# A language-model layer with local and full attention and a mixture of experts, on one core: masks merged, one turn per shift, expert biases in bf16, and the first scores ahead of batch 1's projections

## The chip, the cores and the metric

The kernel runs on one core of a Trainium2 chip. The metric is the device time of one execution in microseconds. Times of before are the median of three runs and one further, profiled execution.

## What is computed

Four sequences of 512 tokens, 256 columns. The embedding rows are gathered; then local attention (16 heads of 16 columns, windows of 128 tokens, each query window sees its own window causally and the one before) on the normalised rows; then, again on normalised rows, full attention with 16 heads plus a mixture of 8 experts of which each token uses 2.

```python
h = W_tok[x]                                      # (4, 512, 256)
h = h + local_attention(layernorm(h)) @ Wo + bo   # window 128, one back, causal
xn = layernorm(h)
q, k, v = split(xn @ W_qkv + b_qkv)
attn = softmax(q @ k.T / sqrt(16)) @ v            # full, 16 heads
gate = softmax(xn @ W_gate + b_gate)
top_g, top_i = top_k(gate, 2)
combine = sum(one_hot(top_i, 8) * top_g[..., None], axis=2)
expert_out = einsum('bsd,edf->bsef', xn, W_experts) + b_experts
h = h + attn + einsum('bsef,bse->bsf', expert_out, combine)
```

## The kernel before

Everything is written by hand in five instruction streams, one per engine, which wait for one another on semaphores. There are eight stages, `STAGES`: local attention of batches 0, 1, 2, full of 0, local of 3, full of 1, 2, 3. Ahead of them stands an opening (`START`) of `START_SLOTS` half slots. A stage has 16 slots (units), 4 groups of 4 heads with 4 key tiles each, and a slot two half slots.

Softmax needs each row's maximum first. So for every head TensorE (PE) computes row scores (`row_scores`, tile SC, two banks) from stacked bf16 parts of q and k: each fp32 value is split in three bf16 parts, and `PRODUCTS` says which parts meet in the 96 rows of QS and KS. In a local stage a bank holds two windows; each window is one matmul (L1487) and one more (L1490) that adds a causal mask by the identity. VectorE (DVE) takes the negated maxima of a bank (`maxima`, L989, L994, L997). When a group of four heads has its maxima, DVE splits them into two bf16 parts (`shift`, L1006, L1008), PE turns them (`turn_shift`, L1419, four transposes, one per row tile, into 8 rows of 512), ScalarE (ACT) copies the bank to shiftT (`copy_shift`, L831), and two DMAs bring shiftT into rows 96 and 97 of QS (`shift_rows`, L515 on SP; for the first group L898 on ACT's queue). Only then can PE compute the transposed scores of that group (`scores`, tile ST, L1504 full, L1510 local), ScalarE takes exponentials (prob, L851, L854), GpSimd masks the local ones (L722), and PE multiplies by V (`times_v`, tile OB, L1531). Row scores run ahead of the transposed ones by `LEAD` heads, 7 or 6. Their place in a slot is given by quarters.

All else is a job: `prep_jobs` says at which step of a batch's preparation (`PREPS` gives the half slot of step 0) PE turns x (`turn_x`, L1296), projects q and k (`project_qk`, L1309, four jobs of two fp32 matmuls of 512 columns) and v (`project_v`, L1324), turns comb, the tokens' weights of the experts (`turn_comb`, L1332), multiplies it by the experts' biases (`expert_bias`, L1339, jobs "eb"), and so on. Jobs use the banks R0 and R1 in turn, and `claim` waits until the reader of the job two before has finished. q and k parts go to memory (`write_parts`, L508) and come back stacked (`stack`, L478). comb is ready at L1073 on DVE, three steps before its turn; `add_biases` (L1128) adds the eb banks to h.

In the opening `START_HEADS` puts row scores of batch 0's first seven heads between the projections of batch 1: heads 0 and 1 in half slot 21, 2 and 3 in 22, then one each. PE runs 8 warming matmuls on the way (`keep_warm`, L1290, fp32, 256 columns), two of them right before stage 0. Group 0's shift is turned in half slot 23.

## Time and profile before

| | us |
|---|---|
| median of 3 runs | 618.83 (614.81 to 619.05) |
| profiled execution | 616.8 |
| its span (first to last instruction) | 615.1 |
| PE busy | 557.4 (91%), granted clock 0.972 |
| DVE busy | 423.3 (69%) |
| ACT busy | 296.1 (48%) |
| GpSimd (POOL) busy | 182.1 (30%) |
| stage 0 begins | 51.4 |
| stages 1 to 7 begin | 103.7, 155.2, 211.6, 281.8, 350.3, 447.3, 534.9 |

A stage begins where the timeline shows its first transposed score. Busy time is the time in which an engine had an instruction under way; PE's matmuls overlap, and an fp32 matmul shows as two. In the timeline and the chain "x4" is a run of four such records. A granted clock of 1 is 2.4 GHz, of 0.5 it is 1.2 GHz.

### The profile page before, as it was taken

To read this page: it belongs to the slowest core of one execution; us is meant where nothing else is said; L and a number is where in the kernel's file an instruction comes from. 1 tells how busy PE (TensorE), PEld (TensorE's weight loads), DVE (VectorE), ACT (ScalarE), POOL (GpSimd) and SP (SyncE) were. 2 spreads that over 40 slices of the span, in tenths; PEclk is the share of its full clock that TensorE was granted. 3 is DMA by queue.
4 is the path that set the end of the run, shared out by engine and by line. 5 is a ranking of instruction groups with operands and counts; after the bars stand their busy time and mean duration, and the time that the engine had idled before them with its cause. 6 is when DMAs were issued, how large, how long until landed. Compare 5 with 4: busy or idle time off the path is not lost.

```text
span 615.1 us, 9977 instructions
## 1 busy us (share of the span) xinstructions
PE 557.4 (91%) x3453; PEld 300.0 (49%) x3453; DVE 423.3 (69%) x941; ACT 296.1 (48%) x558; POOL 182.1 (30%) x237
## 2 busy tenths in 40 slices
PE   3978899989999898898988899989999899999996
PEld 2445555655655343444543455544535555544452
DVE  6867566758687879576577777756876665677842
ACT  0324455546444665475363354524655455444444
POOL 6436544315222501022132133301133341043201
PEclk9998899999899999999896799999999999999999
DMA  6365334224221443351224123403258578223311
GB/s 186 107 197 173 103 117 126 78 63 121 87 87 53 132 125 101 92 152 55 69 85 141 58 68 125 129 19 97 62 167 240 164 235 254 70 60 104 112 52 36
DMA packets 43521, 69.24 MB, mean 113 GB/s; under 512 B 7368, under 2 KB 36688, under 8 KB 40784
## 3 DMA queue, kind: packets, MB, share of 16 engines
q1 hardware_dynamic: 39088, 55.62, 30.2%
q0 software_dynamic: 4224, 12.59, 6.5%
q8 instruction: 28, 0.46, 0.3%
q10 hardware_dynamic: 160, 0.40, 0.2%
q14 instruction: 21, 0.17, 0.1%
HBM read 45.25 MB, written 23.07 MB: 111 GB/s over the span
## 4 chain that ended last, share of the span: by engine, by line
PE 72%; DVE 17%; issue 4%; DMA 2%; ACT 2%; SPq 1%; POOL 1%; DVEq 0%; ACTq 0%
PE OB L1531 13%; PE R L1411 9%; PE R L1309 9%; PE SC L1482 8%; PE ST L1504 6%; PE R L1324 5%; DVE neg_max L989 4%; PE SC L1487 4%; PE R L1397 3%; PE ST L1510 3%; PE R L1426 2%; PE R L1357 2%; PE SC L1490 2%; DVE neg_max L997 2%; PE R L1296 1%
## 5 line engine op out<-in xcount | busy, mean ns | idle before, releaser
L989 DVE TENSOR_REDUCE neg_max<-SC 128x1 f32<-128x512 f32 x256 | 170.9, 686 | 84.8 <-PE SC L1482 84.0
L851 ACT ACTIVATE prob<-ST 128x512 f32<-128x512 f32 x256 | 136.8, 598 | 123.5 <-PE ST L1504 122.9
L1531 PE MATMUL OB<-prob,VS 128*32 128x512 f32 (+2 forms) x1024 | 109.7, 502 | 0.1
L1482 PE MATMUL SC<-KS,QS 96*128 96x512 bf16 x256 | 98.7, 394 | 8.2 <-DVE neg_max L989 6.1
L854 ACT ACTIVATE prob<-ST 128x512 f32<-128x512 f32 (+1 forms) x128 | 68.4, 543 | 73.2 <-PE ST L1510 72.7
L722 POOL TENSOR_SCALAR_AFFINE_SELECT prob<-prob 128x512 f32<-128x512 f32 x64 | 41.0, 642 | 146.1 <-ACT prob L854 145.9
L1504 PE MATMUL ST<-QS,KS 98*128 98x512 bf16 x256 | 78.1, 382 | 2.0 <-ACT prob L851 1.9
L997 DVE TENSOR_REDUCE neg_max<-SC 128x2 f32<-128x512 f32 x64 | 44.0, 688 | 26.1 <-PE SC L1490 26.0
L1487 PE MATMUL SC<-KS,QS 96*128 96x256 bf16 (+1 forms) x256 | 55.3, 270 | 3.7 <-DVE neg_max L994 2.7
L994 DVE TENSOR_REDUCE neg_max<-SC 128x1 f32<-128x128 f32 (+1 forms) x128 | 39.5, 350 | 23.4 <-PE SC L1490 23.2
L1490 PE MATMUL SC<-mask_q,ident_bf 128*128 128x128 bf16 x256 | 51.7, 226 | 0.0
L1482 PEld LDWEIGHTS SC<-KS,QS 96*128 96x128 bf16 x256 | 25.1, 98 | 50.8 <-DVE neg_max L989 33.6
L1510 PE MATMUL ST<-QS,KS 98*128 98x256 bf16 (+1 forms) x256 | 48.5, 273 | 1.2 <-DMA QS<-shiftT 1.2
L708 POOL TENSOR_TENSOR parts<-rest,parts 128x512 bf16<-128x512 f32 x32 | 37.4, 1169 | 40.9 <-ACT parts L797 24.3
L792 ACT ACTIVATE parts<-R,qk_bias 128x512 bf16<-128x512 f32 x32 | 22.0, 687 | 54.9 <-PE R L1309 54.9
L1504 PEld LDWEIGHTS ST<-QS,KS 98*128 98x128 bf16 x256 | 24.6, 98 | 31.9 <-ACT prob L851 11.6
L732 POOL TENSOR_TENSOR h<-h,AO 128x256 f32<-128x256 f32 x15 | 10.9, 727 | 97.9 <-DVE AO L1031 70.3
L1487 PEld LDWEIGHTS SC<-KS,QS 96*128 96x128 bf16 x256 | 25.3, 101 | 28.0 <-DVE neg_max L994 10.9
L1531 PEld LDWEIGHTS OB<-prob,VS 128*32 128x32 f32 x1024 | 20.5, 110 | 37.0 <-issue 34.0
L962 DVE SCALAR_TENSOR_TENSOR rest<-R,qk_bias,parts 128x512 f32<-128x512 f32 x32 | 23.9, 747 | 18.1 <-ACT parts L792 16.4
L1309 PE MATMUL R<-xT_full,w_qkv 128*128 128x512 f32 x64 | 33.0, 608 | 3.0 <-DVE VS L974 3.0
L1151 DVE SCALAR_TENSOR_TENSOR h<-R,comb,h 128x256 f32<-128x256 f32 x64 | 27.8, 475 | 8.8 <-PE R L1411 8.8
(148 smaller groups left out, 800.5 us busy)
## 6 DMA issues: line engine op xcount, KB each, us to landing
scratch<-parts SPq DMA_DIRECT2D x96, 128.0 KB
QS<-scratch SPq DMA_DIRECT2D x42, 256.0 KB, 3.3
KS<-scratch SPq DMA_DIRECT2D x42, 256.0 KB, 3.6
...
```

The source lines that it names most:

```text
L851: act.activation(prob[:, u % 2, e, :], src[:, :], ACT.Exp, scale=SCALE).then_inc(s_prob, 1)
L854: act.activation(prob_local[:, u % 2, u // 2 % 2, 2 * e:2 * e + 2, 0:w], src[:, :].rearrange("p (i w) -> p i w", i=2)[:, :, 0:w], ACT.Exp, ...
L989: dve.tensor_reduce(own_max[:, i, head:head + 1], bank[:, :], AX.X, ALU.max, negate=True).then_inc(s_max, 1)
L997: dve.tensor_reduce(own_max[:, 2:4, head], bank[:, :].rearrange("p (w k) -> p w k", w=2), AX.X, ALU.max, negate=True).then_inc(s_max, 1)
L1309: mm = pe.matmul(bank[:, :], w, xT_of(p)[:, c, :], start=(c == 0), stop=(c == NC - 1))
L1411: mm = pe.matmul(bank[:, t % 2 * D:(t % 2 + 1) * D], xT_full[b % 2][:, c, t * P:(t + 1) * P], w_exp[n % W_RING][:, c, :], start=(c == 0), ...
L1482: pe.matmul(bank[:, :], Q[0:SHIFT_ROW, head, i * P:(i + 1) * P], K[0:SHIFT_ROW, head, :], start=True, stop=True).then_inc(s_sc_ps, 1)
L1487: pe.matmul(bank[:, first:last], Q[0:SHIFT_ROW, head, w * P:(w + 1) * P], K[0:SHIFT_ROW, head, max(w - 1, 0) * P:(w + 1) * P], start=(w % ...
L1490: mm = pe.matmul(bank[:, last - P:last], ident_bf[:, :], mask_q[:, :], start=False, stop=(w % 2 == 1), skip_group_check=True)
L1504: mm = pe.matmul(bank[:, :], K[0:KROWS, g * GH + e, keys], Q[0:KROWS, g * GH + e, :], start=True, stop=True)
L1510: mm = pe.matmul(bank[:, i * 2 * P:i * 2 * P + w], K[0:KROWS, head, keys], Q[0:KROWS, head, kt * P:kt * P + w], start=(i == 0), stop=(i == 1),
L1531: mm = pe.matmul(OB[VW * i:VW * (i + 1), columns], VS[s % 3][:, kt, v:v + VW], p_of, start=(kt == 0), stop=(kt == NT - 1), skip_group_chec ...
```

## The change

Four things at once.

1. *Masks.* The two mask matmuls of a bank become one of 256 columns (two blocks of 128 with the mask read twice by a stride of 0), after both score matmuls.
2. *Shift.* The two parts are stored as part, head, tile, so that one transpose of 32 columns makes 32 rows of 128; ScalarE copies 32x128; each DMA brings 16 rows of 128 into one row of QS.
3. *Expert biases.* comb and the biases are each split in three bf16 parts; six products of parts are stacked in a contraction of 48 rows, so that turn and product are bf16. comb is split by four GpSimd operations after L1073 (`split_comb`), the biases by four more in stage 0 (`split_biases`), and six DMAs stack them at the start of stage 1. exp_bias now lies in the xs buffers, which are free then.
4. *Opening.* Heads 0 to 3 get half slots 20 to 23, one each, 4 in 24, and 5 and 6 in 25; the shift is turned in 24. Batch 1's projections of q and k are at steps 10, 11, 14, 16 instead of 9, 11, 13, 15, and V at 19 and 21 instead of 14 and 16, the opening is one half slot shorter, and the two warming matmuls before stage 0 go.

```diff
-START_STACK, START_SHIFT = 15, 23
-START_HEADS = {21: (0, 1), 22: (2, 3), 23: (4,), 24: (5,), 25: (6,)}
+START_STACK, START_SHIFT = 15, 24
+START_HEADS = {20: (0,), 21: (1,), 22: (2,), 23: (3,), 24: (4,), 25: (5, 6)}
...
-START_SLOTS, VS_ONES = 27, 5
+START_SLOTS, VS_ONES = 26, 5
...
-Q_STEPS = {"first": (9, 10, 11, 12), "later": (9, 11, 13, 15)}
-V_STEPS = {"first": (13, 14), "second": (14, 16), LOCAL: (10, 12), FULL: (8, 8, 9, 10)}
+Q_STEPS = {"first": (9, 10, 11, 12), "second": (10, 11, 14, 16), "later": (9, 11, 13, 15)}
+V_STEPS = {"first": (13, 14), "second": (19, 21), LOCAL: (10, 12), FULL: (8, 8, 9, 10)}
...
+SPLIT_STEP = 20
+
+BIAS_PRODUCTS = ((0, 0), (0, 1), (0, 2), (1, 0), (1, 1), (2, 0))
...
-        shift = sb("shift", [P, NT, 2 * GH], BF16)
-        shiftT = sb("shiftT", [2 * GH, T], BF16)
+        shift = sb("shift", [P, 2, GH, NT], BF16)
+        shiftT = sb("shiftT", [2 * GH * NT, P], BF16)
...
-                    sp.dma_start(QS[s % 2][SHIFT_ROW + j:SHIFT_ROW + j + 1, g * GH:(g + 1) * GH, :],
-                                 shiftT[j * GH:(j + 1) * GH, :]).then_inc(s_shrow, 16)
+                    sp.dma_start(shift_row(s, g, j), shiftT[j * GH * NT:(j + 1) * GH * NT, :]).then_inc(s_shrow, 16)
...
+            def stack_biases():
+                sp.wait_ge(s_bias_parts, 4)
+                for n, (_, a) in enumerate(BIAS_PRODUCTS):
+                    sp.dma_start(bias_stack[n * E:(n + 1) * E, :], bias_parts[:, a, :]).then_inc(s_bias_stack, 16)
...
+            def split_comb(b):
+
+                n = at(b, 4, 0)
+                pool.wait_ge(s_comb, b + 1)
+                if b > 0:
+                    pool.wait_ge(s_comb_ps, b)
+                rows = comb[b % 2][:, :, :]
+                pool.tensor_copy(comb_parts[:, :, 0:3, :], rows.unsqueeze(2).to_broadcast([P, NT, 3, E]))\
+                    .then_inc(s_comb_parts, 1)
+                pool.wait_ge(s_comb_parts, n + 1)
+                pool.tensor_tensor(comb_rest[:, :, :], rows, comb_parts[:, :, 0, :], ALU.subtract)\
+                    .then_inc(s_comb_parts, 1)
...
             def turn_comb(b):
-                bank = claim(("comb", b, 0))
-                pe.wait_ge(s_comb, b + 1)
+                turned = claim(("comb", b, 0))[:, :].bitcast(BF16)
+                pe.wait_ge(s_comb_parts, at(b, 4, 4))
                 for t in range(NT):
-                    mm = pe.transpose(bank[0:E, t * P:(t + 1) * P], comb[b % 2][:, t, :], ident[:, :])
+                    mm = pe.transpose(turned[0:len(BIAS_PRODUCTS) * E, t * P:(t + 1) * P],
+                                      comb_parts[:, t, :, :].rearrange("p n e -> p (n e)"), ident_bf[:, :])
                 mm.then_inc(s_comb_ps, 1)
...
-                    mm = pe.matmul(bank[:, (t % 2) * D:(t % 2 + 1) * D], combT[:, t * P:(t + 1) * P], exp_bias[:, :],
+                    mm = pe.matmul(bank[:, (t % 2) * D:(t % 2 + 1) * D], combT[:, t * P:(t + 1) * P], bias_stack[:, :],
...
-                for t in range(NT):
-                    mm = pe.transpose(turned[0:2 * GH, t * P:(t + 1) * P], shift[:, t, :], ident_bf[:, :])
-                mm.then_inc(s_shT_ps, 1)
+                pe.transpose(turned[0:2 * GH * NT, 0:P], shift[:, :, :, :].rearrange("p j i t -> p (j i t)"),
+                             ident_bf[:, :]).then_inc(s_shT_ps, 1)
...
-                    mm = pe.matmul(bank[:, last - P:last], ident_bf[:, :], mask_q[:, :], start=False,
-                                   stop=(w % 2 == 1), skip_group_check=True)
-                mm.then_inc(s_sc_ps, 1)
+
+                own = bank[:, :].rearrange("p (w k) -> p w k", w=2)[:, :, (i > 0) * P:((i > 0) + 1) * P]
+                pe.matmul(own, ident_bf[:, :], mask_q[:, :].unsqueeze(1).to_broadcast([P, 2, P]), start=False,
+                          stop=True, skip_group_check=True).then_inc(s_sc_ps, 1)
...
-            keep_warm(2)
             pe.wait_ge(s_ones, 5)
```

PE's stream where the first row scores stand, in the opening, before (R<-ident,xn_local is batch 1's turned x, R<-xT_local,w_q its first q projection, SC<-KS,QS the scores of a window, SC<-mask_q,ident_bf its mask):

```order
L1296 MATMUL R<-ident,xn_local 128x128 x8
L1309 MATMUL R<-xT_local,w_q 128x512 x2
L1487 MATMUL SC<-KS,QS 128x128
L1490 MATMUL SC<-mask_q,ident_bf 128x128
L1487 MATMUL SC<-KS,QS 128x256
L1490 MATMUL SC<-mask_q,ident_bf 128x128
```

The same place in the changed kernel, PE's stream from batch 1's turned x on:

```order
L1355 MATMUL R<-ident,xn_local 128x128 x8
L1548 MATMUL SC<-KS,QS 128x128
L1548 MATMUL SC<-KS,QS 128x256
L1553 MATMUL SC<-mask_q,ident_bf 128x2x128
L1548 MATMUL SC<-KS,QS 128x256 x2
L1553 MATMUL SC<-mask_q,ident_bf 128x2x128
L1368 MATMUL R<-xT_local,w_q 128x512
```

Head 0's two banks now stand ahead of the projection, which comes one matmul at a time between the heads, and a bank has three matmuls instead of four.

PE's stream where the opening ends and stage 0 begins (the first ST rows), before:

```order
L1324 MATMUL R<-w_v,xT_local 128x256 x2
L1309 MATMUL R<-xT_local,w_k 128x512 x2
L1290 MATMUL OB<-w_q,ident 128x256 x2
L1510 MATMUL ST<-QS,KS 128x256 x2
L1324 MATMUL R<-w_v,xT_local 128x256 x2
```

The same place in the changed kernel, PE's stream from the opening's last matmul on:

```order
L1368 MATMUL R<-xT_local,w_q 128x512
L1572 MATMUL ST<-QS,KS 128x256 x2
L1548 MATMUL SC<-KS,QS 128x128
L1548 MATMUL SC<-KS,QS 128x256
L1553 MATMUL SC<-mask_q,ident_bf 128x2x128
L1572 MATMUL ST<-QS,KS 128x256 x2
L1368 MATMUL R<-xT_local,w_k 128x512
```

The last k projection and all of V have moved behind the first transposed scores, the warming matmuls are gone.

SP's stream at the same place (scratch<-parts writes parts of q and k, QS<-shiftT is group 1's shift rows, QS<-scratch and KS<-scratch the stack of batch 1), before:

```order
L478 DMA KS<-scratch 32x1x2048 x3
L508 DMA scratch<-parts 8x16x512 x12
L515 DMA QS<-shiftT 1x4x512 x2
L478 DMA QS<-scratch 32x1x4096
L478 DMA KS<-scratch 32x1x4096
```

The same place in the changed kernel, SP's stream:

```order
L495 DMA KS<-scratch 32x1x2048 x3
L525 DMA scratch<-parts 8x16x512 x6
L532 DMA QS<-shiftT 1x16x128 x2
L495 DMA QS<-scratch 32x1x4096
L525 DMA scratch<-parts 8x16x512 x6
```

Group 1's shift rows, and the first piece of batch 1's stack, now go between the two halves of the parts' writes.

## Rows read from the trace of the kernel before

**Rows 1.** Of the page, part 1: busy us (share of the span) xinstructions.
```profile
PE 557.4 (91%) x3453; PEld 300.0 (49%) x3453; DVE 423.3 (69%) x941; ACT 296.1 (48%) x558; POOL 182.1 (30%) x237
```

**Rows 2.** Of the page, part 4: the chain that ended last, share by engine.
```profile
PE 72%; DVE 17%; issue 4%; DMA 2%; ACT 2%; SPq 1%; POOL 1%; DVEq 0%; ACTq 0%
```

**Rows 3.** Windows, stages 4, 5: PE, PEld, DVE, ACT, POOL, clock, DMA, GB/s.
```profile
281.80:350.30 68.50, 59.32 (x391) 29.98 (x389) 47.27 (x117) 28.04 (x53) 16.66 (x23) 0.83 0.29 89
350.30:447.30 97.00, 93.85 (x488) 51.66 (x485) 70.44 (x156) 45.66 (x86) 23.64 (x25) 0.99 0.27 83
```

**Rows 4.** The timeline, PE: start us, us, engine line op out<-in xcount.
```profile
107.51 0.39 PE L1419 MATMUL R<-ident_bf,shift 128*8 128x128 bf16 x4
107.83 0.23 PE L1487 MATMUL SC<-KS,QS 96*128 96x128 bf16 x1
107.90 0.22 PE L1490 MATMUL SC<-mask_q,ident_bf 128*128 128x128 bf16 x1
107.96 0.27 PE L1487 MATMUL SC<-KS,QS 96*128 96x256 bf16 x1
108.07 0.22 PE L1490 MATMUL SC<-mask_q,ident_bf 128*128 128x128 bf16 x1
```

**Rows 5.** The chain: the first and last of 16 shift turns.
```profile
98.01 0.32 PE R L1419 x4
...
588.63 0.20 PE R L1419 x4
```

**Rows 6.** The timeline, ScalarE and its queue (ACTq), the opening.
```profile
27.80 2.20 ACTq L478 DMA_DIRECT2D KS<-scratch  x3
...
43.14 0.57 ACT L831 COPY shiftT<-R 8x512 bf16<-8x512 bf16 x1
43.74 1.82 ACTq L898 DMA_DIRECT2D QS<-shiftT  x2
```

**Rows 7.** The chain, then the timeline of SP and PE: three times shift rows.
```profile
100.20 3.47 DMA QS<-shiftT
...
103.72 0.39 PE L1510 MATMUL ST<-QS,KS 98*128 98x256 bf16 x2 [1.19 <-DMA QS<-shiftT]
...
108.76 1.19 SPq L515 DMA_DIRECT2D QS<-shiftT  x2
...
111.33 0.38 PE L1510 MATMUL ST<-QS,KS 98*128 98x256 bf16 x2
```

**Rows 8.** The chain: eb jobs, the first, and one at half clock.
```profile
157.54 1.05 PE R L1339 x4
...
289.88 1.87 PE R L1339 x4
```

**Rows 9.** The chain: a turn of comb.
```profile
281.10 0.53 PE R L1332 x4
```

**Rows 10.** Groups of instructions, GpSimd, a small operation.
```profile
L660 POOL TENSOR_SCALAR_AFFINE_SELECT tri<-ones_bf 128x128 bf16<-128x128 bf16 x1 | 0.3, 282 | 0.0
```

**Rows 11.** The timeline, DVE and PE, comb of batch 0.
```profile
152.66 0.19 DVE L1073 TENSOR_TENSOR comb<-chosen,grec 128x32 f32<-128x32 f32 x1
...
153.74 0.60 PE L1332 MATMUL R<-ident,comb 128*8 128x128 f32 x4
```

**Rows 12.** The timeline, PE: a moving operand repeated by a stride of 0.
```profile
340.95 0.35 PE L1371 MATMUL R<-sel,ones_bf 128*128 128x64 bf16 x8
```

**Rows 13.** The timeline, DVE, the opening.
```profile
35.95 0.75 DVE L962 SCALAR_TENSOR_TENSOR rest<-R,qk_bias,parts 128x512 f32<-128x512 f32 x1 [4.35 <-ACT parts L792]
36.62 0.61 DVE L994 TENSOR_REDUCE neg_max<-SC 128x1 f32<-128x128 f32 x2
...
37.78 0.62 DVE L994 TENSOR_REDUCE neg_max<-SC 128x1 f32<-128x128 f32 x2
```

**Rows 14.** The chain, the end of the opening.
```profile
48.97 1.72 PE R L1309 x4
50.69 0.86 PE OB L1290 x4
```

More of the change, by code:

```diff
@@ L204, in q_step @@
 def q_step(p):
-    return Q_STEPS["first" if p == 0 else "later"]
+    return Q_STEPS[("first", "second")[p] if p < 2 else "later"]
 def v_step(p):
@@ L741, in prep @@
                             third_part(p, i)
-                    if what == "local" and step == (26 if p == 0 else q_step(p)[3] + 4):
+                    if what == "local" and step == (24 if p == 0 else q_step(p)[3] + 4):
                         add_bo(b)
+                    if what == "full" and step == SPLIT_STEP:
+                        split_comb(b)
                 if what == "route":
@@ L830, in copy_shift @@
                 turned = bank_of(("shift", group, 0))[:, :].bitcast(BF16)
[L831 removed]
+                act.copy(shiftT[:, :], turned[0:2 * GH * NT, 0:P]).then_inc(s_shT, 1)
             def copy_OT(group):
@@ L1005, in maxima @@
                         dve.wait_ge(s_shT_ps, group)
-                    dve.tensor_copy(shift[:, :, 0:GH], own).then_inc(s_sh1, 1)
+                    first, second = (shift[:, j, :, :].rearrange("p i t -> p t i") for j in (0, 1))
+                    dve.tensor_copy(first, own).then_inc(s_sh1, 1)
                     dve.wait_ge(s_sh1, group + 1)
-                    dve.tensor_tensor(shift[:, :, GH:2 * GH], own, shift[:, :, 0:GH], ALU.subtract)\
-                        .then_inc(s_sh, 1)
+                    dve.tensor_tensor(second, own, first, ALU.subtract).then_inc(s_sh, 1)
             def attention_before(s, g):
```

50 lines of the change are left out of this document (42 added, 8 removed).

## The prediction

> **What bounds the kernel now.** I read the busy shares of the page first: TensorE (PE) is busy 91% of the span [rows 1]. That is an average, so next comes the chain that ended last: 72% of it is PE, 17% VectorE (DVE), 4% bare issue, 2% DMA [rows 2]. Work taken off PE is therefore worth something, but not all of it, since now and then DVE's maxima come last. Then the granted clock by stage: 0.99 in stage 5, where PE is busy 97% of the time, and 0.83 in stage 4, where it is busy 87% [rows 3]. A microsecond of PE's stream saved is worth one where the chain holds the instruction, and little elsewhere.
>
> The sum is made against the profiled execution: 616.8 us, of which the span is 615.1. It lies 2 us under the median of the three timed runs (618.83) and between their extremes.
>
> **One turn per shift.** A group's shift was four bf16 transposes of 128 columns with 8 rows out; now it is one with 32 rows out. Beside one another in the timeline, a matmul of 128 bf16 columns begins 0.06 to 0.07 us before its successor (107.83, 107.90, 107.96), one of 256 columns 0.11 us (107.96, 108.07) [rows 4]. The four transposes begin at 107.51 and the next matmul at 107.83. So three go, 3 x 0.056 = 0.17 us, and the switch-over around them, some 0.1 us, stays. There are 32 such turns, but only 16 stand in the chain, the first at 98.01 and the last at 588.63 [rows 5]: 16 x 0.17 = **2.7 us**. At the other 16 something else came last, and I count nothing for them.
> ScalarE's copy of the turned bank goes from 512 elements, 0.57 us [rows 6], to 128. Bounds for it: the 0.57 itself, and a quarter, 0.14. ScalarE is not the bound (2% of the chain), so this counts only through earlier shift rows. DVE's two small operations on the shift now write with a stride; 16 elements cost what starting an operation costs, and I take 0, ends -0.2 and +1 us.
>
> The shift rows leave as 16 pieces of 128 elements (256 bytes) per DMA where there were 4 of 1 KB. The chain names them once as what PE waited for: 3.47 us after the issue, with 1.19 us of waiting before 103.72 [rows 7]. There the shorter turn and copy give back about 0.5 us, and a slower landing could take it away. Value taken: 0, ends -0.5 and +1; the general case is rival 4.
>
> **Expert biases in bf16.** An eb job is two fp32 matmuls of 256 columns, shown as x4 since each passes twice. Seven of the eight stand in the chain: about 1.05 us each at full clock, 1.87 for the one at half clock [rows 8]. As bf16 each matmul takes the 0.11 us of [rows 4], so a job becomes 2 x 0.11 plus 0.08 of switching = 0.3 us: 6 x 0.75 + (1.87 - 0.6) = **5.8 us**. That the contraction goes from 8 rows to 48 changes nothing in the columns streamed; the scores, with 96 rows, take the same 0.11.
>
> The turn of comb was four fp32 transposes, 0.53 us in the chain [rows 9], four times; as bf16 it is 4 x 0.056 plus the switch, 0.32. 4 x 0.21, and a little more for the one at half clock: **1.0 us**.
>
> What is added is on GpSimd: four small operations after comb, each waiting for the one before. The nearest row is an affine select of 128x128, 0.28 us [rows 10]; four of these with short gaps are 1.3 us. For batches 1 to 3 comb is ready 3 us and more before PE turns it, so this is hidden. For batch 0 DVE ends comb at 152.85 and PE turned it at 153.74 [rows 11]; now it can't before 154.2, and PE takes its instructions in order, so row scores, transposed scores and values stand behind it. **-0.5 us**, ends 0 and -1.2 (each operation half as long, or twice). The four operations that split the biases (stage 0, GpSimd) and the six DMA issues that stack them (start of stage 1, SP, 6 x 0.6 = 3.6 us by the two issues of [rows 7] in 1.19) come while GpSimd has nothing due but a mask every slot, and two slots ahead of SP's next shift rows, some 6 us. I count 0; if the SP ones collide, the next group is late once, 1 us.
>
> **Merged masks.** Per bank two mask matmuls of 128 columns become one of 256. The columns are equal and one instruction's own overhead goes: 0.06 + 0.06 becomes 0.11, about 6 ns a bank. 128 banks, of which two thirds are in PE-bound stretches: **0.5 us**. That a moving operand repeated by a stride of 0 runs at full rate is shown by the routing counts, eight such matmuls within 0.35 us [rows 12]. Bounds: 0 and 1.5.
>
> **The opening.** Before, PE projects batch 1's first q, and DVE sits idle 4.35 us until that projection's remainder at 35.95, ahead of its first maximum at 36.62 [rows 13]. Stage 0 begins at 51.4, after a k projection of 1.72 us and the warming matmuls, 0.86 [rows 14]. Now head 0's scores stand ahead of the projection. They can start when batch 1's transposes have ended, shortly before the projection did, and ScalarE's K stack has landed: issued 27.80 to 30.00 [rows 6], its last piece from 29.3 on, and at most 3.5 us from issue to landing as in [rows 7], so 33 or little earlier. A head costs DVE 37.78 - 36.62 = 1.16 us. Four heads and two remainders of 0.75 end at 33.3 + 6.1 = 39.4, shift ready at 39.8 (it was 42.6). Turn and copy to 40.5, ScalarE issues the two rows until 42.3 (1.82 us [rows 6]), and they land at 43.7 to 45.2 (2.0 or 3.5 us after the second issue begins, by the two cases of [rows 7]). DVE's three further heads and one remainder run until 44.0, PE's last scores a head before that. So stage 0 starts at 44.4, 7.0 us earlier. Of this the k projection (1.72) and V's first four fp32 matmuls twice (0.9 each, as long as the four warming ones of the same size) are owed to stage 0; the warming is really gone. 7.0 - 3.5 = **3.5 us**. Bounds: 1 (DVE's idle time merely moves) and 5.
>
> **Sum.** 2.7 + 5.8 + 1.0 - 0.5 + 0.5 + 3.5 = 13.0 us. Outside the opening DVE often follows closely, and where a microsecond of PE goes the next maximum is late instead; by the share of DVE and issue in the chain I take off a fifth of those 9.5 us, 2.0. Forecast 616.8 - 11.0 = 605.8, rounded to **606 us**.
>
> **Rivals.**
> 1. *DVE takes over.* PE gets its two banks for row scores back from DVE's maxima. If half of the chain terms (9.5) turn into that wait and the opening gives only 1 us and the warming matmuls, it is 616.8 - 4.8 - 1.9 = 610. For it: DVE is 17% of the chain [rows 2]. Against it: bias jobs and turns lie among projections, which give DVE time.
> 2. *More than the sum.* In stage 0 PE waits for DVE again and again and its clock is halved twice for 3.4 us; if both go (up to 1.7 us of stream each) and the opening gives 5, it is about 600.
> 3. *The clock, the slower side.* Less PE work leaves PE idle more often. Stage 4 was granted 0.83 at 87% busy, stage 5 0.99 at 97% [rows 3]. If stage 5 alone fell to stage 4's clock, its 93.9 us of PE would take 93.9 x (0.99/0.83 - 1) = 18 us more, and the time be 616.8 - 11 + 18 = 624. It decides from 0.89 on, where it eats the 11 us. Against it: the idle added there is some 2% of the stage.
> The Trainium skill (TensorE: Matmul & The Clock Gate, "The HAM clock gate") puts it generally: the slow clock is the default and activity releases it. The trace agrees in direction; by that rule a kernel that only loses PE work gains less than the columns say.
> 4. *Late shift rows.* SP ends an issue at 109.95 and PE uses the rows at 111.33 without a recorded wait [rows 7]. Through the timeline five or six of the 32 groups are that tight. If 256-byte pieces landed 2.5 us later, each of these would cost 2 us and the next tight ones some: 12 us, nothing gained, 618. Against it: 4 KB is little in any pieces.
> The Trainium skill (DMA: Bandwidth & Descriptors, Specifications) says that pieces under 512 bytes go by read-modify-write and miss the line rate. No run here shows yet what that is worth for 4 KB.
>
> **Numbers.** Forecast 0.62; rival 1 0.17; rival 2 0.11; rival 3 0.06; rival 4 0.04. The range takes in rival 1's 610 with what lies past it, and rival 2's 600: 599 to 613. A measurement of this kernel tells about 1% from no change, that is 612.6 against the median of 618.8: faster 0.80 (the forecast, rival 2 and half of rival 1), same 0.15, slower 0.05.
>
> **What would show it.** The first score of stage 0 near 44.4; DVE's 4.35 us idle before its first maximum down to about 1.5; an eb job 0.3 us and a turned shift 0.15 in the chain; less than 1 us of waiting at batch 0's turn of comb; at most one wait for shift rows over 1 us; stages 1 to 7 shorter by 0.5 to 2 us each. Wrong if PE's waits for maxima grow by over 5 us, if the granted clock after 350 us falls below 0.97, or if stage 0 starts before 46 and its end still comes less than 2 us earlier.

## The result, and the profile after

The changed kernel takes 602.85 us (median of 4 runs, 601.53 to 603.44) against 618.11 for the kernel before: a ratio of 0.975, 95% interval 0.970 to 0.979. In experiment e5 the same kernel took 603.71 against 618.66, ratio 0.976 (0.971 to 0.981). Over its ten runs the median is 603.1. The forecast was 606, within 599 to 613. Two runs, one of e11 with 658.2 us (granted clock 0.835) and one of the kernel before with 1338.5 us beside e5 to e8, lie far above all others and are left out of the medians below.

The profiled execution is 602.96 us with a span of 601.2. First the page of the changed kernel, busy times and then the chain by engine, for [rows 1, 2]:

```profile
PE 538.9 (90%) x3209; PEld 282.9 (47%) x3209; DVE 424.4 (71%) x941; ACT 285.4 (47%) x558; POOL 188.2 (31%) x257
...
PE 67%; DVE 20%; issue 5%; DMA 4%; ACT 2%; SPq 1%; POOL 1%; ACTq 0%; DVEq 0%
```

PE lost 244 instructions and 18.5 us of busy time, more than the span lost (13.9), and DVE's share of the chain went from 17 to 20%.

Then the windows by stage, from one first ST matmul to the next (start:end, length, PE, PEld, DVE, ACT, POOL busy, granted clock, DMA share, GB/s). The kernel before, the opening, stage 0 and stage 2; its stages 4 and 5 are [rows 3]:

```profile
0.00:51.39 51.39, 35.85 (x152) 20.98 (x153) 34.95 (x66) 13.71 (x22) 27.38 (x48) 1.00 0.57 168
51.39:103.72 52.33, 46.99 (x390) 27.76 (x388) 35.30 (x84) 25.96 (x51) 27.65 (x36) 0.93 0.43 132
155.18:211.62 56.44, 52.42 (x397) 29.90 (x393) 41.49 (x94) 27.22 (x52) 18.61 (x26) 0.97 0.27 83
```

The changed kernel, the same three and stages 4 and 5:

```profile
0.00:50.78 50.78, 33.74 (x120) 18.60 (x121) 34.63 (x64) 11.31 (x19) 27.38 (x48) 0.93 0.58 167
50.78:101.08 50.30, 46.33 (x358) 26.85 (x356) 36.62 (x87) 26.31 (x53) 29.65 (x40) 1.00 0.46 140
152.45:205.55 53.10, 48.58 (x363) 26.87 (x359) 41.36 (x92) 25.92 (x52) 18.59 (x26) 1.00 0.29 86
275.00:338.19 63.19, 51.82 (x354) 24.94 (x352) 46.98 (x117) 26.54 (x53) 17.62 (x27) 0.89 0.32 97
338.19:435.64 97.45, 94.22 (x477) 51.50 (x473) 70.21 (x156) 44.50 (x86) 24.63 (x29) 0.98 0.27 83
```

The gain sits in a few places: the opening 0.6 us, stage 0 2.0, stage 1 0.1, stage 2 3.3, stage 3 0.7, stage 4 5.3, stage 5 -0.5, stages 6 and 7 2.2 together. The clock column must be read with the length. The kernel before ran at half clock (1.2 instead of 2.4 GHz) for 6.8 us of stage 0, 3.4 of stage 2 and 22.6 of stage 4. The changed one has none in stages 0 and 2 and 13.8 in stage 4, but 6.8 in the opening, where there was none. So a good part of the differences between stages is the clock's. And part of that is not the change's: in the second profile of the changed kernel (e5) stage 4 had 20.6 us at half clock and was 65.6 us long, a gain of 2.9 instead of 5.3, while its opening had none.

The new operations in the chain of the changed kernel (start us, us, what), a turn of the shift, the first turn of comb and two eb jobs, for [rows 5, 8, 9]:

```profile
95.90 0.23 PE R L1480
151.13 0.38 PE R L1391 x4
154.79 0.32 PE R L1401 x2
```

An eb job is 0.32 to 0.39 us where it was 1.05 to 1.87, and a turned shift 0.04 to 0.26, in the chain 15 times.

### The profile page after: what moved, and what is told of

It reads as the page before. It is cut to its first block, busy times and chain, and to the rows that moved or that the text cites. A ratio compares the mean times of both kernels' runs of the same rounds, so it can differ in the third digit from the quotient of the medians.

```text
span 601.2 us, 9518 instructions
## 1 busy us (share of the span) xinstructions
PE 538.9 (90%) x3209; PEld 282.9 (47%) x3209; DVE 424.4 (71%) x941; ACT 285.4 (47%) x558; POOL 188.2 (31%) x257
## 4 chain that ended last, share of the span: by engine, by line
PE 67%; DVE 20%; issue 5%; DMA 4%; ACT 2%; SPq 1%; POOL 1%; ACTq 0%; DVEq 0%
PE OB L1593 12%; PE R L1473 9%; PE R L1368 9%; PE SC L1543 8%; PE ST L1566 6%; DVE neg_max L1048 6%; PE R L1383 4%; PE SC L1548 3%; PE R L1459 3%; PE R L1487 2%; PE R L1419 2%; PE ST L1572 2%; DVE neg_max L1056 2%; PE SC L1553 2%; DVE stats L991 1%
## 5 line engine op out<-in xcount | busy, mean ns | idle before, releaser
L1593 PE MATMUL OB<-prob,VS 128*32 128x512 f32 (+2 forms) x1024 | 107.7, 493 | 0.1
L1548 PE MATMUL SC<-KS,QS 96*128 96x256 bf16 (+1 forms) x256 | 47.4, 268 | 3.9 <-DVE neg_max L1053 1.8
L1543 PEld LDWEIGHTS SC<-KS,QS 96*128 96x128 bf16 x256 | 24.9, 97 | 54.6 <-DVE neg_max L1048 38.1
L1572 PE MATMUL ST<-QS,KS 98*128 98x256 bf16 (+1 forms) x256 | 46.8, 264 | 0.5 <-DMA QS<-shiftT 0.5
L1566 PEld LDWEIGHTS ST<-QS,KS 98*128 98x128 bf16 x256 | 24.8, 98 | 32.2 <-ACT prob L909 11.8
L1548 PEld LDWEIGHTS SC<-KS,QS 96*128 96x128 bf16 x256 | 21.2, 100 | 36.7 <-issue 16.9
L1553 PE MATMUL SC<-mask_q,ident_bf 128*128 128x256 bf16 x128 | 36.0, 281 | 0.0
L1572 PEld LDWEIGHTS ST<-QS,KS 98*128 98x128 bf16 x256 | 25.4, 100 | 18.2 <-issue 11.5
```

Source lines behind the costliest of these rows:

```text
L1543: pe.matmul(bank[:, :], Q[0:SHIFT_ROW, head, i * P:(i + 1) * P], K[0:SHIFT_ROW, head, :], start=True, stop=True).then_inc(s_sc_ps, 1)
L1548: pe.matmul(bank[:, first:last], Q[0:SHIFT_ROW, head, w * P:(w + 1) * P], K[0:SHIFT_ROW, head, max(w - 1, 0) * P:(w + 1) * P], start=(w % ...
L1553: pe.matmul(own, ident_bf[:, :], mask_q[:, :].unsqueeze(1).to_broadcast([P, 2, P]), start=False, stop=True, skip_group_check=True).then_in ...
L1566: mm = pe.matmul(bank[:, :], K[0:KROWS, g * GH + e, keys], Q[0:KROWS, g * GH + e, :], start=True, stop=True)
L1572: mm = pe.matmul(bank[:, i * 2 * P:i * 2 * P + w], K[0:KROWS, head, keys], Q[0:KROWS, head, kt * P:kt * P + w], start=(i == 0), stop=(i == 1),
L1593: mm = pe.matmul(OB[VW * i:VW * (i + 1), columns], VS[s % 3][:, kt, v:v + VW], p_of, start=(kt == 0), stop=(kt == NT - 1), skip_group_chec ...
```

## The experiments

Six runs each, twelve for e12. The kernel before had a median of 618.2 us beside e1 to e4, 618.7 beside e5 to e8, 617.8 beside e9 to e12. The runs of one kernel lie up to 9 us apart, so a difference of two medians is good to about 2 or 3 us; what happened in a stage is read from the traces. The starts of four stages in the profiled executions (first ST matmul of each, us), and where half clock fell (start, length) up to 200 us:

| kernel | median | stage 0 | stage 1 | stage 3 | stage 5 | half clock |
|---|---|---|---|---|---|---|
| before | 618.1 | 51.4 | 103.7 | 211.6 | 350.3 | 58.0 (3.4), 64.8 (3.4), 163.8 (3.4) |
| changed | 602.9 | 50.8 | 101.1 | 205.5 | 338.2 | 34.3 (3.4), 44.5 (3.4) |
| e1 old opening | 604.2 | 50.8 | 101.8 | 206.3 | 338.9 | 59.3 (3.4) |
| e2 four turns | 605.3 | 49.9 | 100.4 | 205.1 | 339.2 | 42.0 (6.8) |
| e3 fp32 biases | 610.2 | 49.6 | 100.2 | 208.8 | 343.0 | 42.0 (6.8), 158.0 (6.8) |
| e4 masks apart | 607.2 | 49.4 | 101.1 | 207.5 | 341.4 | 44.5 (6.8) |
| e5 changed again | 603.7 | 47.2 | 98.2 | 202.9 | 338.2 | none |
| e6 two heads first | 602.1 | 49.0 | 99.5 | 205.4 | 338.8 | 34.9 (3.4), 45.2 (3.4), 198.8 (3.4) |
| e7 warm in waits | 600.3 | 47.5 | 98.8 | 203.2 | 337.7 | none |
| e8 bias of 8 rows | 604.8 | 51.1 | 101.4 | 205.9 | 341.9 | 34.6, 44.9 (3.4 each) |
| e9 stage 4 filled | 605.1 | 47.3 | 98.4 | 202.9 | 341.9 | none |
| e10 two heads and warm | 600.3 | 45.6 | 96.8 | 203.3 | 335.9 | 195.7 (6.8) |
| e11 biases alone | 611.3 | 54.5 | 106.5 | 211.8 | 347.1 | 33.1, 39.9, 67.2 (3.4 each) |
| e12 opening alone | 614.7 | 49.4 | 100.2 | 209.6 | 347.4 | 42.8 (3.4), 158.9 (6.8) |

**e1, the old opening in the changed kernel.**

```diff
-START_STACK, START_SHIFT = 15, 24
-START_HEADS = {20: (0,), 21: (1,), 22: (2,), 23: (3,), 24: (4,), 25: (5, 6)}
+START_STACK, START_SHIFT = 15, 23
+START_HEADS = {21: (0, 1), 22: (2, 3), 23: (4,), 24: (5,), 25: (6,)}
```

with the old START_SLOTS, Q_STEPS and V_STEPS and keep_warm(2) before stage 0.

> The changed kernel with the old opening (heads two at a time from half slot 21, batch 1's V at 14 and 16, two warming matmuls before stage 0). In the profile of the changed kernel stage 0 starts only 0.6 us earlier than before, not 7, and stage 1 2.6 us earlier. Theory A (the new opening is worth what stage 1's start shows): 602.9 + 2.6 minus the masks and turns of stage 0 (0.5) = 605.0, and its own half-clock stretches lie in stage 0 again (58 and 65 us), not in the opening. Theory B (the opening is worth nothing; what stage 1's start shows came by the other three parts and by luck of the clock): 602.9 to 603.5. Theory C (the old opening would now be better, because PE and DVE stand idle together for 3 us in the new one): 601 or less.

Measured: 604.24 (601.24 to 608.74), ratio to before 0.980 (0.976 to 0.983): 1.1 us over the changed kernel's 603.1, less than the runs can settle. In its trace stage 0 starts at the same 50.8, stage 1 0.7 later. What the new opening is worth must come from more traces (below, at the opening).

**e2, four turns per shift.**

```diff
-                pe.transpose(turned[0:2 * GH * NT, 0:P], shift[:, :, :, :].rearrange("p j i t -> p (j i t)"),
-                             ident_bf[:, :]).then_inc(s_shT_ps, 1)
+                for t in range(NT):
+                    mm = pe.transpose(turned[0:2 * GH, t * P:(t + 1) * P], shift[:, t, :], ident_bf[:, :])
+                mm.then_inc(s_shT_ps, 1)
```

> The changed kernel with four transposes per shift, the copy of 8x512 and DMAs of 4 x 1 KB. Chain theory (only the 16 turns that stand in the chain count): +2.7 us, 605.6. Stream theory (all 32 count): +5.4 us, 608.3. Latency theory (the shorter copy and landing matter too, by earlier shift rows where PE waits for them): stage 1's start is 0.5 us later beyond the turns, total +3.5 to +6. If 256-byte pieces land later than 1 KB pieces, the wait before stage 1's first score is shorter here than the one of 3.4 us after the issue ends in the changed kernel.

Measured: 605.31 (603.99 to 606.94), ratio 0.980 (0.977 to 0.983), 2.2 us more. Group by group its trace is 0.11 to 0.25 us longer in eleven of the 32 groups, 1.75 us together, and the same within 0.1 us in the others, except for groups 18 (1.1 more), 22 (1.0), 26 (0.4) and 27 (0.25 less). Group 18 was 1.1 us longer in e5 too, with no edit, so these four say nothing of the turns. So a turn costs what its rows said where PE's stream is the bound, and nothing elsewhere.

**e3, fp32 expert biases.** exp_bias, combT of 8 rows and the fp32 turn of comb again, no split and no stacking:

```diff
-                    mm = pe.matmul(bank[:, (t % 2) * D:(t % 2 + 1) * D], combT[:, t * P:(t + 1) * P], bias_stack[:, :],
+                    mm = pe.matmul(bank[:, (t % 2) * D:(t % 2 + 1) * D], combT[:, t * P:(t + 1) * P], exp_bias[:, :],
```

> The changed kernel with the expert biases and the turn of comb in fp32, without the splitting operations. Theory A (stream): eb jobs and comb turns come back with 5.8 + 1.0 - 0.5 = +6.3 us, 609.2. Rival (half of it turned into waits for DVE): +3, 606. In the profile an eb job is 1.05 us in the chain again, against about 0.3.

Measured: 610.18 (607.59 to 610.75), ratio 0.987 (0.983 to 0.990), 7.1 us more. PE's eb rows of e3, and the window of its group 8:

```profile
153.42 1.13 PE L1349 MATMUL R<-exp_bias,combT 8*128 8x256 f32 x4
157.46 1.55 PE L1349 MATMUL R<-exp_bias,combT 8*128 8x256 f32 x4 [0.99 <-DVE AO L1041]
...
151.15:165.06 13.91, 12.82 (x90) 7.72 (x87) 7.57 (x20) 5.86 (x12) 2.54 (x4) 0.75 0.25 78
```

and the same of the changed kernel:

```profile
154.72 0.39 PE L1401 MATMUL R<-bias_stack,combT 48*128 48x256 bf16 x2
158.03 0.39 PE L1401 MATMUL R<-bias_stack,combT 48*128 48x256 bf16 x2 [0.99 <-DVE AO L1090]
...
152.45:161.81 9.36, 8.34 (x85) 5.35 (x82) 7.33 (x18) 5.77 (x12) 2.16 (x4) 1.00 0.31 89
```

Group 8 is 4.5 us longer. Two jobs of 0.75 us more each explain 1.5; the other 3 fit the 6.8 us at half clock from 158.0 on. The wait of 0.99 us for DVE stands in both. Group 24, which holds two more such jobs, is 3.1 us longer with 3.4 us at half clock from 451.6 on. Half clock stood in group 8 in all three traces with fp32 biases (before, e3, e12) and in none of the eleven others.

**e8, the biases on 8 rows.** Leaves out five of the six products: only the first 8 of the 48 stacked rows are contracted.

```diff
-                    mm = pe.matmul(bank[:, (t % 2) * D:(t % 2 + 1) * D], combT[:, t * P:(t + 1) * P], bias_stack[:, :],
+                    mm = pe.matmul(bank[:, (t % 2) * D:(t % 2 + 1) * D], combT[0:E, t * P:(t + 1) * P], bias_stack[0:E, :],
```

> The changed kernel with the bias product over the first 8 of the 48 stacked rows only; five of the six products of parts are left out. Columns and instruction count are the same. In e3 with fp32 biases of 8 rows the clock was halved for 6.8 us around the eb jobs of stage 2, and here it was not. If that hangs on how few rows of PE the eb matmuls fill, a half-clock stretch comes back in stage 2 and its first group takes 12 us and more; if it hangs on the time that fp32 takes and the waits around it, group 8 takes 9.4 us as now and the time is 602.9.

Measured: 604.82 (601.28 to 608.33). PE's first eb row and the window of group 8:

```profile
155.08 0.39 PE L1401 MATMUL R<-bias_stack,combT 8*128 8x256 bf16 x2
...
152.81:162.18 9.37, 8.36 (x86) 5.35 (x83) 7.33 (x18) 5.77 (x12) 2.17 (x4) 1.00 0.28 85
```

Rows of contraction changed neither the job nor the clock of group 8. What counted there was fp32 against bf16, not 8 rows against 48.

**e4, masks apart.** After each window's scores again a mask matmul of 128 columns of its own:

```diff
-                pe.matmul(own, ident_bf[:, :], mask_q[:, :].unsqueeze(1).to_broadcast([P, 2, P]), start=False,
-                          stop=True, skip_group_check=True).then_inc(s_sc_ps, 1)
+                    mm = pe.matmul(bank[:, last - P:last], ident_bf[:, :], mask_q[:, :], start=False,
+                                   stop=(w % 2 == 1), skip_group_check=True)
+                mm.then_inc(s_sc_ps, 1)
```

> The changed kernel with two mask matmuls per bank. By columns: +0.5 us (6 ns at 128 banks, two thirds of them where PE is the bound), 603.4, not to be told from no change. Rival: each matmul costs more than its columns (its weight load, its instruction): +3 us or more.

Measured: 607.15 (603.49 to 609.23), ratio 0.983 (0.979 to 0.987), 4.1 us more. Its trace is 3.2 us longer than the changed kernel's, with an opening 1.4 us shorter. The longer groups are of three kinds. Thirteen groups are 0.05 to 0.33 longer, 1.6 us together, which I take for the columns' own price. Groups 0 and 16 are 1.0 and 0.7 longer with more half clock (group 16 was 1.25 longer in e5, with no edit). Group 4 is 1.4 longer because group 5's shift rows, issued from 105.8 on, came late. PE's wait in e4:

```profile
109.92 0.39 PE L1571 MATMUL ST<-QS,KS 98*128 98x256 bf16 x2 [1.19 <-DMA QS<-shiftT]
```

That wait is in no other trace of the series (group 4 is 7.4 to 7.6 us long in all of them, 8.8 here). The same rows, issued at the same time, were used 2.1 us after the second issue's begin in the changed kernel and 3.5 us here; one trace doesn't tell whether masks apart bring it. The masks are worth 1.6 us by the groups and perhaps up to 4 by the medians, which is not shown.

**e5, the changed kernel again**, unedited, to see what of its opening repeats.

> The changed kernel itself, on the same chip and in the same hour as the next three. All theories: 602.9, within 601.5 to 604.5, stages as in its first profile except where a half-clock stretch falls otherwise (up to 1.7 us each).

Measured: 603.71 (599.33 to 607.11). PE's wait for the shift and the window up to stage 0, in e5:

```profile
42.65 0.22 PE L1480 MATMUL R<-ident_bf,shift 128*32 128x128 bf16 x1 [3.16 <-DVE shift L1068]
...
28.00:47.20 19.20, 13.41 (x71) 7.34 (x70) 14.34 (x30) 3.83 (x7) 12.14 (x20) 1.00 0.64 190
```

and in the first profile of the same kernel:

```profile
44.67 0.26 PE L1480 MATMUL R<-ident_bf,shift 128*32 128x128 bf16 x1 [3.15 <-DVE shift L1068]
...
28.00:50.78 22.78, 16.52 (x72) 8.63 (x71) 14.46 (x30) 3.83 (x7) 12.03 (x20) 0.85 0.67 192
```

The same work and the same wait of 3.15 us, but the clock 1.00 in the one and 0.85 in the other, and 3.5 us between the starts of stage 0. One execution of the same kernel differs here from another by more than the two openings differ in the mean (2.6 us, below). The lead didn't last: the spans are 601.2 and 601.4 us. e5 gave 0.7 us back in stage 0 and 2.4 in stage 4, where it had the more half clock.

**e6, two heads first.**

```diff
-START_HEADS = {20: (0,), 21: (1,), 22: (2,), 23: (3,), 24: (4,), 25: (5, 6)}
+START_HEADS = {20: (0, 1), 21: (2,), 22: (3,), 23: (4,), 24: (5,), 25: (6,)}
```

> The changed kernel with two heads ahead of the first projection of batch 1 (START_HEADS 20: 0 and 1, 21: 2, 22: 3, 23: 4, 24: 5, 25: 6) and the shift still turned in half slot 24, so that head 4's scores no longer stand behind a turn that waits. Theory A (what holds the new opening back is DVE without row scores: 1.3 us before head 1, 1.1 us before head 4, 1.4 us before head 5, and remainders waited for ahead of maxima): the shift is ready near 40.6 instead of 44.5, stage 0 starts 3 us or more earlier, and the time falls by 2 to 3 us to about 600.5. Theory B (the opening is bound by PE's own stream at the granted clock and by what stage 0 owes anyway): stage 0 may start earlier, but stage 1 starts at 101 as before, 603.

Measured: 602.06 (598.45 to 604.35), ratio 0.971 (0.967 to 0.976). That is 1.0 us under the changed kernel's 603.1, less than the runs can settle. DVE's shift is ready at 42.8 instead of 44.5 and stage 0 starts 1.7 us earlier, with two stretches of half clock as in the changed kernel. DVE's waits between the heads shrank only from 2.95 to 2.4 us (1.27, 1.23 and 0.45 before, rows below, at the opening). Another 0.7 us came because the second remainder now stands behind the shift, and 0.8 because the two operations on the shift themselves ran faster. DVE in e6, then GpSimd (POOL) in e6, then GpSimd in the changed kernel, where the same two operations took 0.52 and 0.65 us from 43.32 on:

```profile
42.34 0.19 DVE L1066 CAST shift<-neg_max 128x16 bf16<-128x16 f32 x1
42.56 0.20 DVE L1068 TENSOR_TENSOR shift<-neg_max,shift 128x16 bf16<-128x16 f32 x1
...
43.31 1.15 POOL L731 TENSOR_TENSOR parts<-rest,parts 128x512 bf16<-128x512 f32 x1 [7.07 <-ACT parts L855]
...
43.07 2.77 POOL L738 TENSOR_TENSOR h<-h,o_bias 128x256 f32<-128x256 f32 x4
```

In e6 GpSimd is idle beside them, in the changed kernel it adds. The new layout of the shift isn't the reason: e12 has the old layout and the new order, and its two operations take 0.51 and 0.65 us.

**e7, warm matmuls in the opening's waits.**

```diff
                 if t == WARM_X:
                     keep_warm(2)
+                if t == 20:
+                    keep_warm(3)
+                if t == 24:
+                    keep_warm(6)
```

> The changed kernel with warming matmuls where PE waits in the opening: three ahead of head 0 (half slot 20), six ahead of the turn of shift 0 (half slot 24). Clock theory (the two half-clock stretches of the opening, at 34 and 44 us, follow PE's waits, and cost it what the new order saves): no half-clock stretch before stage 0, stage 0 starts 1.5 to 3 us earlier, 600.5 to 601.5. Rival (DVE is the bound of the opening, the clock of PE costs nothing there): the stretches go, and the start of stages 0 and 1 moves less than 0.5 us, 603.

Measured: 600.29 (599.35 to 601.39), ratio 0.969 (0.966 to 0.973). The opening has no half clock, stage 0 starts at 47.5, and the median is 2.8 us under the changed kernel's 603.1. All six runs lie within 2.1 us, those of e5 within 7.8; but the first four runs of the changed kernel lay within 1.9 too, so the smaller spread is not shown. PE's wait for the shift went from 3.15 to 0.57 us. Of the seven profiles with the new opening and no remedy, six had half clock in the opening.

**e9, stage 4's waits filled as well.** On top of e7, and likewise 6 matmuls ahead of an eb job and 7 ahead of group 18's turn of O:

```diff
+            def fill(bank, n):
+                for _ in range(n):
+                    pe.matmul(bank[:, 0:P], ident[:, :], ident[:, :], start=True, stop=True)
...
             def turn_shift(group):
-                turned = claim(("shift", group, 0))[:, :].bitcast(BF16)
+                bank = claim(("shift", group, 0))
+                fill(bank, {17: 16, 20: 7}.get(group, 0))
+                turned = bank[:, :].bitcast(BF16)
```

> The kernel of warm matmuls in the opening's waits, and besides: where PE waits for DVE in stage 4 and just before stage 5 it multiplies the identity by itself meanwhile (16 times 128 fp32 columns ahead of group 17's turn of shift, 6 ahead of the second expert bias job of batch 1, 7 ahead of group 18's turn of O, 7 ahead of group 20's turn of shift), in banks that are overwritten next. Nothing of the computation changes. Before it these four waits took 2.27, 0.94, 1.06 and 0.97 us, and stretches at half clock of 6.8 us followed at 279 and at 334. Theory that PE's waits bring the half clock and the half clock costs time there: both stretches go, stage 4 is 60 to 62 us long (65.1 before it), the time 3 to 5 us under the other kernel with warm matmuls (600.3), 596. Rival, DVE is the bound there whatever PE's clock: the stretches may go, but the next maxima come last, stage 4 is 64.5 to 65.5 long, the time within 1 us of 600.3. Second rival: the matmuls outlast the waits and delay the turns; PE's stream grows by 1 us, 601.

Measured: 605.11 (604.06 to 607.97), 4.8 us slower than e7. PE in e9, the fill and its turn, then the window of group 16:

```profile
278.99 3.84 PE L1481 MATMUL R<-ident 128*128 128x128 f32 x32 [2.27 <-DVE h L1187]
282.76 0.23 PE L1488 MATMUL R<-ident_bf,shift 128*32 128x128 bf16 x1
...
272.28:289.33 17.05, 14.17 (x123) 10.02 (x121) 10.62 (x32) 5.50 (x12) 4.51 (x7) 1.00 0.26 76
```

and e7:

```profile
279.36 0.29 PE L1480 MATMUL R<-ident_bf,shift 128*32 128x128 bf16 x1 [2.27 <-DVE h L1187]
...
272.64:286.75 14.11, 10.90 (x80) 5.67 (x77) 10.31 (x32) 5.57 (x12) 4.54 (x7) 0.76 0.29 91
```

The fill stands behind the wait, not in it. The row said so: it names DVE's h (L1187), which reads the bank that the turn claims, and not DVE's shift (L1068). PE waited for a free bank, and so no matmul into that bank can fill the wait. The stretch at half clock after it did go (clock 1.00 instead of 0.76). Since 16 and 6 fp32 matmuls cost 5.4 us there and a wait of 0.94 us behind them went, and the group grew by only 2.9, the half clock had cost some 1.6 us, by this estimate. Group 19, which holds the other two fills, grew by 2.7 us; groups 18 and 20 came out 1.1 shorter each. Whether a fill inside the wait pays wasn't tried: it needs another bank.

**e10, two heads first and three warm matmuls** (the edits of e6, and of e7 at t == 20).

> The changed kernel with two heads' scores (instead of one) ahead of the first half of the second q projection, and three warm matmuls after them; nothing left out. Two heads alone gave 602.1 and warm matmuls alone 600.3, against 603.3 for the changed kernel (mean of its two medians). Theory that the two remedies are of different kinds (DVE's early work, PE's clock) and add up: stage 0 starts at 46.0 to 46.8, no half clock in the opening, time 599 to 599.5. Rival, both remove the same half-clock stretches: stage 0 starts at 47.2 or later, the time is 600 to 601.

Measured: 600.33 (597.76 to 601.96), ratio 0.971 (0.967 to 0.975). Stage 0 starts at 45.6, 1.9 before e7, yet the medians are equal. In the profiled executions the lead is gone where stage 3 begins, and the profile shows where it went. PE in e10:

```profile
193.35 0.39 PE L1543 MATMUL SC<-KS,QS 96*128 96x512 bf16 x1 [0.71 <-DVE neg_max L1048]
195.98 0.61 PE L1543 MATMUL SC<-KS,QS 96*128 96x512 bf16 x1 [0.75 <-DVE neg_max L1048]
...
196.00:200.00 4.00, 4.00 (x20) 1.96 (x21) 1.91 (x3) 0.85 (x2) 2.69 (x5) 0.50 0.09 33
```

and in e7:

```profile
195.32 0.39 PE L1543 MATMUL SC<-KS,QS 96*128 96x512 bf16 x1 [0.71 <-DVE neg_max L1048]
197.96 0.39 PE L1543 MATMUL SC<-KS,QS 96*128 96x512 bf16 x1 [0.75 <-DVE neg_max L1048]
...
198.00:202.00 4.00, 3.66 (x32) 1.66 (x32) 3.27 (x7) 1.51 (x4) 3.12 (x6) 1.00 0.12 38
```

The same two waits at the same place of the program; after them half clock in e10, full in e7, and group 11 is 14.75 us long in the one, 12.73 in the other. Half clock in group 11 stands in both traces with two heads first (e6, 14.15 us, and e10) and in none of the twelve others, so it may belong to this order of the heads; two traces don't settle it. The profiled execution of e10 was 599.98 us long all the same, that of e7 601.39, for e10's stage 4 was 1.9 us shorter, with 13.9 us at half clock against 21.1.

**e11, the biases alone, and e12, the opening alone**, each put into the kernel before, with nothing else changed. e11 makes the edits that e3 undoes:

```diff
-                    mm = pe.matmul(bank[:, (t % 2) * D:(t % 2 + 1) * D], combT[:, t * P:(t + 1) * P], exp_bias[:, :],
+                    mm = pe.matmul(bank[:, (t % 2) * D:(t % 2 + 1) * D], combT[:, t * P:(t + 1) * P], bias_stack[:, :],
```

> The kernel before with the bf16 expert biases alone (split, stacked, bf16 turn of comb); masks, turns and opening as before. Theory that the biases are worth 7 us wherever they stand, clock included: 611.2 (610 to 612.5) against 618.2, group 8 shortened from 12.5 to 9.4 us and without a half-clock stretch. By my prediction's terms alone (5.8 + 1.0 - 0.5 less a fifth) 5.1 us: 613. Rival, half of the gain came only together with the other parts: 614.5 to 616.

Measured: 611.34 (611.22 to 613.27, 5 runs), ratio 0.990 (0.986 to 0.994): 6.5 us. Group 8 is 9.43 us long (12.47 before) with no half clock, groups 16, 18 and 24 are 1.3 to 1.5 shorter. Its opening, which the edit doesn't touch, had two stretches at half clock and ended at 54.5, 3.1 later than in the profile of before.

e12 makes those that e1 undoes:

```diff
-START_HEADS = {21: (0, 1), 22: (2, 3), 23: (4,), 24: (5,), 25: (6,)}
+START_HEADS = {20: (0,), 21: (1,), 22: (2,), 23: (3,), 24: (4,), 25: (5, 6)}
```

> The kernel before with the new opening alone (order of the scores, slots of the projections, START_SHIFT and V steps of the second preparation); masks, four turns and fp32 biases as before. By my prediction's term 3.5 us: 614.7. Theory after undoing it in the changed kernel (0.5 to 1.3 us worth): 617 to 617.7, stage 0 starts at 49.5 to 51, where half-clock stretches fall in the opening again, or near 47 where none does. Rival, slower since V's and k's work lands in stage 0: 619 to 621.

Measured: 614.67 (612.45 to 621.48, 12 runs), ratio 0.995 (0.992 to 0.998): 3.1 us, with an interval from 1 to 5. PE's first turn in e12:

```profile
43.12 0.58 PE L1430 MATMUL R<-ident_bf,shift 128*8 128x128 bf16 x4 [3.19 <-DVE shift L1019]
```

The same long wait as in the changed kernel, and 3.4 us at half clock from 42.8 on. Stage 0 starts 2.0 us earlier than in the profile of before and is 1.5 us shorter, although it now holds a k projection and V's matmuls on top. Stage 2 has 6.8 us at half clock behind its fp32 jobs and gives 1.4 back.

## Why the prediction was right, and where not

**The sum.** Undone one at a time, the parts are worth 1.1 (opening), 2.2 (turns), 7.1 (biases) and 4.1 (masks), 14.5 together; the whole is 618.2 - 603.1 = 15.1. The forecast said 13.0 for the parts and took off 2.0. Each of these is good to 2 or 3 us only, so the agreement doesn't show that the parts add up: with the masks and turns by their groups (1.6 and 1.7) the four come to 11.5. The term that has no support is the *cover of a fifth*, 2.0 us: PE's waits for maxima didn't grow (below). Without it the forecast would have been 603.8. What no term of the sum held is the clock's stretches going away: the trace of before has 34.8 us at half clock, the two of the changed kernel 24.3 and 24.4, and 10.4 us less are worth at most 5.2. In group 8 that goes with the fp32 biases (e3). In stage 0 it goes with the old opening: its three traces (before, e1, e11) have half clock in stage 0, and of the eleven with the new order only e4, whose stretch began in the opening. In stage 4 it changes from execution to execution, 13.8 and 20.6 us in the same kernel. Rival 2 named stage 0's.

**Biases: right.** Forecast 5.8 + 1.0 - 0.5 = 6.3; measured 6.5 alone and 7.1 undone. A job came out at 0.32 to 0.39 us (0.3). The sum held no clock, and in e3 about 3 us of group 8 and 1.6 of group 24 are more than the columns' price, so some of the other places gave less than counted. Which ones wasn't worked out.

**GpSimd's split: right.** PE's turn of comb for batch 0 waits for it, in the changed kernel:

```profile
149.50 0.19 DVE L1132 TENSOR_TENSOR comb<-chosen,grec 128x32 f32<-128x32 f32 x1
149.76 0.27 POOL L767 CAST comb_parts<-comb 128x96 bf16<-128x96 f32 x1 [0.37 <-DVE comb L1132]
...
150.74 0.24 POOL L776 TENSOR_TENSOR comb_parts<-comb_rest,comb_parts 128x32 bf16<-128x32 f32 x1
...
151.13 0.38 PE L1391 MATMUL R<-ident_bf,comb_parts 128*48 128x128 bf16 x4 [0.51 <-POOL comb_parts L776]
```

0.51 us, as priced, and the four operations take 1.2 us. The other split, of the biases in stage 0, was counted as 0 and is not quite free: it runs beside one pair of shift operations on DVE, which take 0.70 and 0.42 us there, and 0.19 and 0.20 in e3, which has no split.

**One turn per shift: right.** Forecast 2.7 in 16 places; 2.2 by the medians, 1.7 in eleven groups of the traces.

**Masks: undersized.** Forecast 0.5, measured 1.6 by the groups of e4. I had counted 6 ns a bank, with eight banks to a group 0.05 us, yet thirteen groups grew by 0.12 in the mean. By the medians (4.1) it may be more, which stays open, and so does whether the late rows of e4 belong to it.

**Shift rows: the term held, but the landing is later.** SP's queue and PE's use of group 4's rows in the changed kernel, for [rows 7]:

```profile
96.45 1.22 SPq L532 DMA_DIRECT2D QS<-shiftT  x2
97.70 4.24 SPq L571 DMA_DIRECT2D bias_stack<-xs  x6
...
101.08 0.39 PE L1572 MATMUL ST<-QS,KS 98*128 98x256 bf16 x2 [0.51 <-DMA QS<-shiftT]
```

and PE's use of them in e5, the same kernel:

```profile
98.21 0.39 PE L1572 MATMUL ST<-QS,KS 98*128 98x256 bf16 x2 [1.20 <-DMA QS<-shiftT]
```

One wait, 0.5 us in the one and 1.2 in the other, where it was 1.2; in e7, whose stage 0 starts early as in e5, it is 1.5. So part of what an earlier stage 0 gains is waited for here again. Rival 4, 2.5 us on each of five or six groups, didn't come. But the landing did become later. PE waits for these rows in all fourteen traces, and from the second issue's begin to PE's use it is 3.4 to 3.7 us in the four with pieces of 1 KB (before, e2, e11, e12) and 4.0 to 5.0 in the ten with 256 bytes. The six stacking DMAs right behind are not the reason: e11 has them and 3.4 us, e3 lacks them and has 4.45. The Trainium skill (DMA: Bandwidth & Descriptors, Specifications) warns of pieces under 512 bytes; the traces agree in direction, with 0.3 us or more at this one place.

**The opening: the result near, the working wrong, and so luck.** The step that failed is "Four heads and two remainders of 0.75 end at 33.3 + 6.1 = 39.4, shift ready at 39.8", and with it stage 0 at 44.4. The changed kernel, DVE and then PE:

```profile
34.02 0.62 DVE L1053 TENSOR_REDUCE neg_max<-SC 128x1 f32<-128x128 f32 x2 [2.79 <-PE SC L1553]
36.51 0.62 DVE L1053 TENSOR_REDUCE neg_max<-SC 128x1 f32<-128x128 f32 x2 [1.27 <-PE SC L1553]
39.08 0.75 DVE L1021 SCALAR_TENSOR_TENSOR rest<-R,qk_bias,parts 128x512 f32<-128x512 f32 x1 [1.23 <-ACT parts L850]
43.32 0.52 DVE L1066 CAST shift<-neg_max 128x16 bf16<-128x16 f32 x1
43.87 0.65 DVE L1068 TENSOR_TENSOR shift<-neg_max,shift 128x16 bf16<-128x16 f32 x1
...
33.53 0.34 PE L1548 MATMUL SC<-KS,QS 96*128 96x128 bf16 x2 [1.48 <-DMA KS<-scratch]
```

DVE starts at 34.0 (33.3 forecast) since the K stack lands 4.49 us after its issue, not 3.5. It then waits for PE between the heads, 1.27, 1.23 and 0.45 us (0.25, 0.71 and 0.45 in e5, at full clock), where I had run it without a gap, and its two operations on the shift take 1.2 us where I allowed 0.4, because GpSimd adds beside them (e6). The shift is ready at 44.5; in e7, at full clock, at 42.7. PE meanwhile waits 3.15 us for it. With half clock before and behind this wait stage 0 starts at 50.8, with none (e5) at 47.2. Even that is 2.8 us later than forecast.

The second step that failed is that the k projection and V's matmuls "are owed to stage 0", 3.5 us. Stage 0 holds them now, but it didn't grow: 52.3 us before, 50.8 in e12, which has the new opening alone. Before had 6.8 us of it at half clock, e12 none, and PE stood idle for 5.3 us of it before, for 3.2 in e12. Over the profiles with the new opening and no remedy (changed, e2, e3, e4, e5, e8, e12) stage 0 starts at 49.6 in the mean and stage 1 at 100.4; with the old one (before, e1, e11) at 52.2 and 104.0. That is 2.6 and 3.6 us, though the mean of the second is of three traces only and both sets mix kernels with other parts changed. So 2.6 us less nothing stood where 7.0 less 3.5 was forecast, two errors that cancel. e12's 3.1 us agree with the forecast's 3.5; e1's 1.1 doesn't contradict it.

**What would have shown it wrong.** PE's waits by releaser (us in total, times, longest), the kernel before:

```profile
PE SC L1482 <- DVE neg_max L989: 6.1, 13, 1.1
PE SC L1487 <- DVE neg_max L994: 2.7, 4, 1.5
```

and the changed one:

```profile
PE SC L1543 <- DVE neg_max L1048: 6.9, 15, 1.1
PE SC L1548 <- DVE neg_max L1053: 1.8, 7, 0.4
```

Together they went from 8.8 to 8.7 us, so rival 1, DVE taking over with 4.8 us, didn't come. Rival 3, a falling clock, neither: after 338 us it was 0.98 to 1.00 in every stage, and stage 4's went from 0.83 to 0.89, in e5 to 0.84. The Trainium skill's rule behind it (TensorE: Matmul & The Clock Gate, "The HAM clock gate") holds here in direction, since every half-clock stretch whose rows are shown above follows waits of PE; but taking fp32 work away did not add to them. "Stages 1 to 7 shorter by 0.5 to 2 us each" failed: stage 1 gained 0.1, its group 7 being 0.4 longer with the wait for the split of comb, stages 2 and 4 gained 3.3 and 5.3 with the clock, stage 5 lost 0.5. DVE's idle time before its first maximum, 4.35 us, was to come down to 1.5 and came to 2.8 (2.3 in e5).
